# A second attention reordered: q and k first, v in the banks of scores, small work at other places

## The chip, the cores and the metric

The kernel runs on one NeuronCore of a Trainium2 chip. TensorE (PE) multiplies matrices and transposes, VectorE (DVE), ScalarE (ACT) and GpSimd (POOL) work on tiles, and SyncE (SP) only issues DMAs. Each engine takes its instructions in program order, and engines wait for one another by semaphores. SBUF holds tiles of 128 partitions; PE writes to PSUM, eight banks of 128x512 fp32. The metric is the time of one execution on the device in microseconds (us), the median of several.

## The reference

Four layers, each with a residual, on x of 8 sequences of 512 tokens, 256 wide:

```
x = x + attn_a(layernorm(x))     # 16 heads of 64, ALiBi, causal
x = x + ffn(layernorm(x))        # RMS norm, gate, top 2 of 8 experts, swiglu
x = x + attn_b(layernorm(x))     # 8 heads of 128
x = x + ffn(layernorm(x))        # the same weights again

attn_b:  q, k, v = x @ w_aq, x @ w_ak, x @ w_av      # 256 -> 8 heads of 128
         q, k = rope(q), rope(k)                     # rotary positions
         s = q k^T / 128 - 1e30 * (key after query)
         o = softmax(s) v ;   r = o @ w_ao           # 8 heads of 128 -> 256

ffn gate: logits = h @ gate_w.T + gate_b ; vals, idx = top_k(logits, 2)
          wts = softmax(vals)
```

The tokens are then sorted by expert. Only attn_b, the second attention, is changed, and with it the places at which the gate of the layer behind it is computed.

## The kernel before

The program has four stages, one behind the other: `attention_a`, `experts(0)`, `attention_b`, `experts(1)`. In each stage every engine has a function that issues its instructions in an order written out by hand; there is no scheduler. The change lies in `attention_b` (lines 1231 to 1957).

One **unit** is one head of one sequence: u runs from 0 to 63, sequence bt = u // 8, head p = u % 8. I call the units of a sequence its first (p = 0) to its eighth (p = 7). What is done for a head:

- PE `proj_qk` (L1310 to L1312): q (j = 0) and k (j = 1) for 512 tokens, six matmuls each, since every fp32 operand is split into a high and a low part in fp32r. Into bank 0 and bank 1.
- DVE `rope` (L1695 to L1697): three multiplications by the tables out of the bank into `rp`. This frees the bank. POOL `rope` (L1866) adds the two halves into `rf`.
- ACT `high` (L1502) rounds `rf` to the high part, POOL `low` (L1873) takes the rest.
- PE `scores` (L1356 to L1358): four blocks of 128 queries, t = 3 (512 keys) down to t = 0, into banks 2 and 3 in turn; blocks 1 and 0 share the bank of block 3, and wait until DVE has read that.
- DVE `maxima` (L1704): adds the mask, takes the row's maximum, writes P to SBUF. ACT `exps` (L1519), DVE `invert` (L1712), ACT `scale` (L1529), which divides by the sum.
- PE `turn_p` (L1372): P is transposed in three parts, into banks 4 and 5; ACT `copy_p` (L1539) brings each to SBUF.
- PE `attend` (L1387): P times V into bank 6; ACT `heads` (L1545) copies it to `OT`.

The work is pipelined over units. In turn u of the loop PE does the scores of unit u + 1, the transposes of unit u between them, the q and k of unit u + 3, and `attend` of unit u. ACT does in turn u: `copy_p` of u, `high` of u + 2, `exps` and `scale` of u + 1, `heads` of u. DVE does the `maxima` of u + 1 and the `rope` of u + 3, with `invert(u + 1)` between its halves.

Once for four heads PE projects v as well (`proj_v`, L1330 to L1332, four blocks of 128 tokens, six matmuls each, into banks 0 and 1), which ACT copies (L1508). That falls into the second and the sixth unit of a sequence, which are longer on PE by it. In the first unit PE also does `outproj` (L1407) of the sequence before, in two halves through bank 7.

Between these stands the **small work** of a sequence, for the gate of the layer behind it and for the input of the next sequence:

- `residual`, `stats`, `gather_stats`, `normal` on DVE with `deviation` and `mean_square` on POOL: the norms; ACT `gate_in` (L1554, four activations) writes `hh`.
- `gate_turn` (PE, L1282, one part for each half of the features) transposes `hh` into bank 7, ACT `gate_high` (L1561) copies each part, PE `gate_logits` (L1423).
- `top_two` in five pieces (DVE, L202 to L228) and `route` in five (DVE, L264 to L279), with ACT `ratio` (L1574), which the last piece of `top_two` needs; PE `rank`; POOL `put_ids` (L292), four DMAs behind one another, needs the last piece of `route`.
- `xpose` (PE), `x_high` (ACT, L1495) and `x_low` (DVE, L1685): the transposed input of the next sequence. All of `proj_qk` and `proj_v` of that sequence need it; the first of them is the v block in the sixth unit.
- ACT `weigh` (L1569, eight activations) and POOL `combine` (L1859): the layer's input two sequences ahead.

Where the small work stands is set by p in the loops of PE, ACT and POOL. On DVE it is set by a number `at = 7 * p + s` in `between(u, s)`: s = 0 to 3 is behind the four `maxima`, s = 4 behind them, before `rope`, s = 5 and 6 behind `rope`. In the last sequence (bt = 7) the pieces of `listing` and `places` stand there too.

## Time and profile before

| | us |
|---|---|
| median of 3 runs | 2345.34 (2340.38 to 2346.77) |
| the profiled execution, its own time | 2350.32 |
| its span in the trace | 2348.5 |
| PE busy over the span | 2140.3 (91%) |
| DVE busy | 1530.3 (65%) |
| ACT busy | 1453.8 (62%) |
| POOL busy | 1288.9 (55%) |
| the second attention, from the first projection to the first matmul of the experts behind it | 1236.7 to 2056.0 |
| PE's busy time in 100 us of its middle (1657 to 1757) | 93.82 |

The second attention is a bit over a third of the span. A row of the timeline reads: start in us from the span's start, duration, engine, line, operation, tiles; in brackets how long the engine stood idle before it and for whom. The names of tiles are those of the program without their numbers, so `q` stands for all four parts of q and k, `stage` for the transposed gate input, `bank` for any PSUM bank.

### The profile page before, as it was taken

To read this page: it belongs to the slowest core of one execution; us is meant where nothing else is said; L and a number is where in the kernel's file an instruction comes from. 1 tells how busy PE (TensorE), PEld (TensorE's weight loads), DVE (VectorE), ACT (ScalarE), POOL (GpSimd) and SP (SyncE) were. 2 spreads that over 40 slices of the span, in tenths; PEclk is the share of its full clock that TensorE was granted. 3 is DMA by queue.
4 is the path that set the end of the run, shared out by engine and by line. 5 is a ranking of instruction groups with operands and counts; after the bars stand their busy time and mean duration, and the time that the engine had idled before them with its cause. 6 is when DMAs were issued, how large, how long until landed. Compare 5 with 4: busy or idle time off the path is not lost.

```text
span 2348.5 us, 38389 instructions
## 1 busy us (share of the span) xinstructions
PE 2140.3 (91%) x11652; PEld 1722.6 (73%) x11652; DVE 1530.3 (65%) x4317; ACT 1453.8 (62%) x3769; POOL 1288.9 (55%) x1450
## 2 busy tenths in 40 slices
PE   6999999999999999898987999999999999899993
PEld 5677777777777776677875777777777778677882
DVE  5767676767676858466755666656665666656665
ACT  4877676868686868343434776757676575634443
POOL 3665555555555545566643546565665655456661
PEclk8999999999999999999998999999999999899996
DMA  3320000000000001333331001001010000522426
GB/s 124 109 99 28 1 28 1 28 1 28 1 28 1 19 3 69 122 101 100 126 117 37 19 10 37 28 18 46 1 45 28 1 19 3 207 64 72 158 88 237
DMA packets 55140, 132.34 MB, mean 56 GB/s; under 512 B 12256, under 2 KB 30208, under 8 KB 53920
## 3 DMA queue, kind: packets, MB, share of 16 engines
q1 hardware_dynamic: 37216, 92.58, 10.7%
q0 software_dynamic: 17728, 37.32, 5.8%
q8 instruction: 102, 1.67, 0.3%
q14 instruction: 94, 0.77, 0.1%
HBM read 81.51 MB, written 48.35 MB: 55 GB/s over the span
## 4 chain that ended last, share of the span: by engine, by line
PE 59%; DVE 12%; ACT 11%; POOL 8%; issue 6%; DMA 3%; SPq 0%; ACTq 0%; POOLq 0%; DVEq 0%
PE bank L619 5%; PE bank L641 5%; PE bank L2086 4%; PE bank L601 3%; PE bank L1407 3%; PE bank L1387 3%; PE bank L586 2%; PE bank L2060 2%; PE bank L2061 2%; PE bank L2062 2%; ACT P L1519 2%; ACT P L763 2%; PE bank L1372 2%; PE bank L587 2%; ACT P L1529 2%
## 5 line engine op out<-in xcount | busy, mean ns | idle before, releaser
L1107 POOL TENSOR_TENSOR P<-P,rc 128x128 f32<-128x128 f32 (+3 forms) x512 | 355.0, 724 | 361.7 <-DVE rc L929 361.4
L921 DVE CUSTOM_DVE_ANT_0 P<-bank,tab 128x512 f32<-128x512 f32 (+3 forms) x512 | 241.7, 486 | 130.0 <-PE bank L587 126.3
L763 ACT ACTIVATE P<-P,mn 128x128 f32<-128x128 f32 (+3 forms) x512 | 281.5, 552 | 47.7 <-DVE mn L921 44.6
L774 ACT COPY PT<-bank 128x512 f32<-128x512 f32 (+1 forms) x384 | 193.9, 516 | 102.6 <-PE bank L601 95.2
L1873 POOL TENSOR_TENSOR q<-rf,q 128x512 fp32r<-128x512 f32 x128 | 162.4, 1291 | 170.2 <-ACT q L1502 170.1
L1866 POOL TENSOR_TENSOR rf<-rp 128x512 f32<-128x512 f32 x128 | 163.3, 1277 | 165.3 <-DVE rp L1697 161.4
L601 PE MATMUL bank<-cst,P 128*128 128x128 f32 x1280 | 207.8, 277 | 30.3 <-ACT PT L774 16.5
L2290 POOL DMA_INDIRECT yD<-Yf,place x142 | 139.3, 981 | 140.1 <-ACT Yf L2150 128.8
L586 PE MATMUL bank<-q 128*128 128x512 f32 (+3 forms) x512 | 186.7, 375 | 18.8 <-DVE mn L921 14.4
L2136 ACT ACTIVATE sgf<-glf 128x256 f32<-128x256 f32 x142 | 59.3, 418 | 230.3 <-DVE glf L2207 230.3
L601 PEld LDWEIGHTS bank<-cst,P 128*128 128x128 f32 x1280 | 152.8, 141 | 61.3 <-ACT PT L774 21.6
L897 DVE TENSOR_TENSOR q<-bank,q 64x512 fp32r<-64x512 f32 x256 | 175.8, 687 | 8.7 <-ACT q L754 2.6
L310 POOL DMA_INDIRECT Gf<-hD,idx x142 | 138.6, 976 | 67.5 <-issue 40.4
L1519 ACT ACTIVATE P<-P,mn 128x128 f32<-128x128 f32 (+3 forms) x256 | 140.9, 553 | 47.4 <-DVE mn L1704 47.4
L1704 DVE CUSTOM_DVE_ANT_0 P<-bank,tab 128x512 f32<-128x512 f32 (+3 forms) x256 | 117.8, 485 | 72.8 <-PE bank L1358 72.1
L619 PE MATMUL bank<-PT,V 128*64 128x512 f32 (+3 forms) x1024 | 154.4, 444 | 9.1 <-DVE xTl L887 8.2
L754 ACT CAST q<-bank 64x512 fp32r<-64x512 f32 x256 | 146.7, 573 | 13.3 <-PE bank L534 10.2
L587 PE MATMUL bank<-q 128*128 128x512 f32 (+3 forms) x512 | 154.4, 327 | 0.0
L1539 ACT COPY PT<-bank 128x512 f32<-128x512 f32 (+1 forms) x192 | 94.4, 517 | 96.8 <-PE bank L1372 96.1
L1387 PE MATMUL bank<-PT,V 128*128 128x512 f32 (+3 forms) x512 | 152.8, 442 | 0.9 <-ACT PT L1539 0.9
L1529 ACT ACTIVATE P<-P,rc 128x128 f32<-128x128 f32 (+3 forms) x256 | 123.0, 552 | 49.4 <-DVE rc L1712 49.4
L2086 PE MATMUL bank<-W2f,ATf 128*128 x568 | 148.5, 384 | 0.0
(230 smaller groups left out, 6001.4 us busy)
## 6 DMA issues: line engine op xcount, KB each, us to landing
hD<-hh SPq DMA_DIRECT2D x16, 512.0 KB, 2.6
W1lf<-w1lD SPq DMA_DIRECT2D x2, 4096.0 KB, 13.1
yg<-yD SPq DMA_DIRECT2D x14, 512.0 KB, 4.6
X<-in_x SPq DMA_DIRECT2D x8, 512.0 KB, 4.4
stage<-in_w SPq DMA_DIRECT2D x8, 512.0 KB, 3.5
w1hD<-W1A SPq DMA_DIRECT2D x8, 512.0 KB, 2.7
w1lD<-stage SPq DMA_DIRECT2D x8, 512.0 KB, 3.6
rD<-xn SPq DMA_DIRECT2D x8, 512.0 KB, 2.9
```

The source lines that it names most:

```text
L586: e.matmul(o, QS[:, k, hl, ts], KS[:, k, hl, 0:w], start=True, stop=False)
L587: i = e.matmul(o, QS[:, k, hl, ts], KL[:, k, hl, 0:w], start=False, stop=True)
L601: i = e.transpose(o[:, at:at + 128], P[:, h % 3, OFF[t] + cc * 128:OFF[t] + cc * 128 + 128], ident)
L619: i = e.matmul(bank[6][64 * hl:64 * hl + 64, cc * 128:512], V[:, g % 2, cc, col:col + 64], PT[:, hl, PTO[cc]:PTO[cc] + w], start=cc == 0, ...
L763: i = e.activation(ps, ps, ACT.Exp, bias=mn[:, pb, t:t + 1], scale=-1.0, accum_out=rs[:, pb, t:t + 1])
L774: e.copy(PT[:, h % 2, PTO[cs[0]]:PTO[cs[0]] + w], bank[4 + n % 2][:, 0:w]).then_inc(q.a_pt, 1)
L897: e.tensor_tensor(L, bank[j][own, :], H.bitcast(F32), ALU.subtract).then_inc(v_q, 1)
L921: e.tensor_tensor_reduce(out=P[:, pb, OFF[t]:OFF[t] + w], in0=score(h, t), in1=tab[:, 512 - w:512], scale=-SLOPES[h % 16], scalar=3e38, op ...
L1107: i = e.tensor_tensor(ps, ps, rc[:, h % 3, t:t + 1].broadcast_to([128, w]), ALU.mult)
L1387: i = e.matmul(bank[6][:, cc * 128:512], V[:, g % 2, cc, col:col + 128], PT[:, u % 2, PTO[cc]:PTO[cc] + w], start=cc == 0, stop=cc == TT - 1)
L1519: i = e.activation(ps, ps, ACT.Exp, bias=mn[:, pb, t:t + 1], scale=-1.0, accum_out=rs[:, pb, t:t + 1])
L2086: i = e.matmul(o, AT[:, k, kc], W2[:, ex, kc].rearrange("p x n -> p (x n)"), start=False, stop=kc == 1)
```

## The change

The list, in the order of the diff below:

1. **Opening of the stage.** PE first projects q and k of head 0, then v blocks 0 and 1, q and k of head 1, v blocks 2 and 3. These four v blocks go to banks 2, 3, 4 and 5 (`v_bank`), which scores and transposes use later, instead of taking turns in banks 0 and 1; scores and transposes of unit 0 now wait for the copies. ACT copies two v blocks, then `high(0)`, two more, then `high(1)`, which stood behind `exps(0)`. The projection of head 2 and its `rope` stand before the loop, behind the scores of unit 0.
2. **Gate.** `gate_in` goes from the third unit to the second (ACT), `gate_turn(0)` from the fourth unit to the third, `gate_turn(1)` from the end of the fourth unit to between its scores and transposes, `gate_logits` from the fifth unit to the fourth (PE); `gate_high` follows (ACT).
3. **ratio** goes from the fifth unit to the sixth, `weigh` from the second to the first (except in sequence 0).
4. **DVE.** `top_two` 1 to 3 and `route` 0 and 1 go together to `at = 39`, behind the maxima of the sixth unit and before its `invert`; `top_two` 4 to `at = 40`, behind the `rope` of that unit; `route` 2 and 3 together to 46, `route` 4 from 48 to 53, in the eighth unit before its `rope`. `x_low(0)` goes from the end of the fifth unit into the sixth, behind its second maximum, `x_low(1)` behind its fourth. In sequence 0, `normal` goes from 17 and 18 to 24 and 25, one unit later.
5. **POOL.** `deviation` for the input goes from the first unit, behind `put_ids` and `low`, to the eighth unit of the sequence before, ahead of `put_ids`.

```diff
@@ -1300,7 +1305,9 @@
                             e.wait_ge(v_wlo, 12 + SPLIT_AT[2 * j + p // 4])
-                        if u % 4 == 0:
+                        if u == 0:
+                            e.wait_ge(q.v_xT, turned(0, 1))
+                        elif u % 4 == 0:
                             e.wait_ge(a_v, u + 3 + j)
@@ -1320,11 +1327,11 @@
                             e.wait_ge(q.v_xT, turned(bt, 1))
-                        if t > 1:
+                        if g and t > 1:
                             e.wait_ge(a_v, 4 * g + t - 1)
...
                             e.wait_ge(v_rp, 2 * (4 * g - 1) + t + 1)
-                        o, ts = bank[t % 2][:], slice(t * 128, (t + 1) * 128)
+                        o, ts = v_bank(g, t)[:], slice(t * 128, (t + 1) * 128)
                         for kc in range(2):
@@ -1347,6 +1354,8 @@
                             e.wait_ge(p_lo, 2 * u + 2)
+                        if u == 0 and t > 1:
+                            e.wait_ge(a_v, 4 - t)
                         if t == 3 and u:
@@ -1366,6 +1375,8 @@
                             e.wait_ge(q.a_pt, n - 1)
+                        else:
+                            e.wait_ge(a_v, n + 3)
                         at = 0
@@ -1432,10 +1443,17 @@
                                 i.then_inc(q.m_x, 1)
-                    proj(0)
-                    proj(1)
+                    for j in range(2):
+                        proj_qk(0, j)
+                    proj_v(0, 0)
+                    proj_v(0, 1)
+                    for j in range(2):
+                        proj_qk(1, j)
+                    proj_v(0, 2)
+                    proj_v(0, 3)
                     for t in (3, 2, 1, 0):
                         scores(0, t)
+                    proj(2)
                     for u in range(NU):
@@ -1448,9 +1466,9 @@
                                 rank(e, 1, bt - 1)
+                            if p == 3 and bt:
+                                gate_turn(bt - 1, 1)
                             turn_p(u, 0)
-                            if p == 4 and bt:
-                                gate_logits(bt - 1)
                             if p == 5 and nx:
@@ -1462,8 +1480,6 @@
                             outproj(bt - 1, 0)
-                        if u == 0:
-                            proj(2)
                         if u + 3 < NU:
@@ -1474,13 +1490,13 @@
                             pick(e, 1, 0)
-                        if p == 3 and bt:
+                        if p == 2 and bt:
                             if bt == NB - 1:
...
                             gate_turn(bt - 1, 0)
+                        if p == 3 and bt:
+                            gate_logits(bt - 1)
                         attend(u)
-                        if p == 3 and bt:
-                            gate_turn(bt - 1, 1)
                         if p == 4 and nx:
@@ -1576,12 +1592,14 @@
                     x_high(0, 1)
-                    for t in range(TT):
-                        v_copy(0, t)
+                    v_copy(0, 0)
+                    v_copy(0, 1)
                     high(0)
+                    v_copy(0, 2)
+                    v_copy(0, 3)
+                    high(1)
                     exps(0, 0)
                     exps(0, 1)
-                    high(1)
                     scale(0)
@@ -1591,8 +1609,12 @@
                         copy_p(u, 2)
-                        if u and u + 2 < NU:
+                        if p == 3 and bt:
+                            gate_high(bt - 1, 1)
+                        if u + 2 < NU:
                             high(u + 2)
+                        if p == 0 and bt and bt + 2 < NB:
+                            weigh(bt + 2)
                         v = u + 3 < NU and (u + 3) % 4 == 0
@@ -1605,21 +1627,17 @@
                             v_copy((u + 3) // 4, 3)
-                        if u == 0:
-                            high(2)
                         if u + 1 < NU:
                             scale(u + 1)
-                        if p == 4 and bt:
+                        if p == 5 and bt:
                             ratio(bt - 1)
+                        if p == 1 and bt:
+                            gate_in(bt - 1)
                         if p == 2 and bt:
-                            gate_in(bt - 1)
-                        if p == 3 and bt:
                             gate_high(bt - 1, 0)
-                        if p == 1 and bt + 2 < NB:
-                            weigh(bt + 2)
+                        if p == 1 and bt == 0:
+                            weigh(2)
                         heads(u)
-                        if p == 3 and bt:
-                            gate_high(bt - 1, 1)
                         if p == 4 and nx:
@@ -1732,14 +1750,21 @@
                                 normal(1, bt - 1, 2 * (at - 10) + 1)
-                            elif at in (29, 30, 31, 32, 33):
-                                top_two(e, q, at - 29, bt - 1, lg, v8, i8, if8, dv)
-                            elif at == 37:
+                            elif at == 29:
+                                top_two(e, q, 0, bt - 1, lg, v8, i8, if8, dv)
+                            elif at == 39:
+                                for n in (1, 2, 3):
+                                    top_two(e, q, n, bt - 1, lg, v8, i8, if8, dv)
                                 route(e, q, 1, bt - 1, 0)
+                                route(e, q, 1, bt - 1, 1)
                             elif at == 40:
-                                route(e, q, 1, bt - 1, 1)
-                            elif at in (46, 47, 48):
-                                route(e, q, 1, bt - 1, at - 44)
+                                top_two(e, q, 4, bt - 1, lg, v8, i8, if8, dv)
+                            elif at == 46:
+                                route(e, q, 1, bt - 1, 2)
+                                route(e, q, 1, bt - 1, 3)
+                            elif at == 53:
+                                route(e, q, 1, bt - 1, 4)
                         if bt == NB - 1:
@@ -1762,9 +1787,9 @@
                                 gather_stats(0, 1)
-                            elif at in (17, 18):
-                                normal(0, 1, 2 * (at - 17))
-                                normal(0, 1, 2 * (at - 17) + 1)
+                            elif at in (24, 25):
+                                normal(0, 1, 2 * (at - 24))
+                                normal(0, 1, 2 * (at - 24) + 1)
@@ -1783,21 +1808,20 @@
                     invert(0)
+                    rope(2, 0)
+                    rope(2, 1)
                     for u in range(NU):
...
                                 maxima(u + 1, t)
-                                if p == 5 and nx and t == 2:
-                                    x_low(bt + 1, 1)
+                                if p == 5 and nx and t in (2, 0):
+                                    x_low(bt + 1, 1 - t // 2)
                                 between(u, 3 - t)
...
                             residual(bt - 1, 0)
-                        if u == 0:
-                            rope(2, 0)
-                            rope(2, 1)
@@ -1881,16 +1903,12 @@
                     low(1)
+                    rope(2, 0)
+                    rope(2, 1)
                     for u in range(NU):
                         bt, p = divmod(u, 8)
-                        if u and u + 2 < NU:
+                        if u + 2 < NU:
                             low(u + 2)
-                        if p == 0 and bt and bt + 1 < NB:
-                            deviation(0, bt + 1)
-                        if u == 0:
-                            rope(2, 0)
-                            rope(2, 1)
-                            low(2)
                         if p == 2 and bt == 0:
@@ -1906,6 +1924,8 @@
                                 gather(e, 1, q, a)
+                        if p == 7 and bt + 2 < NB:
+                            deviation(0, bt + 2)
                         if p == 7 and bt and bt + 1 < NB:
...
                                 put_ids(e, 1, bt - 1, n)
```

The rows below are the instructions of one engine in the order of the program, numbered, with the tiles they write and read and their shapes.

ACT at the opening of the stage; `xTh` is the transposed input, `q_1` q and k, `P` the scores. Before:

```order
1308 L1495 CAST xTh<-bank 128x512 x2
1309 L1508 COPY V<-bank 128x512 x4
1310 L1502 CAST q_1<-rf 128x512 x2
1311 L1519 ACT_TABLE_LOAD
1312 L1519 ACTIVATE P,rs<-P,mn 128x128
1313 L1519 ACTIVATE P,rs<-P,mn 128x256
1314 L1519 ACTIVATE P,rs<-P,mn 128x384
1315 L1519 ACTIVATE P,rs<-P,mn 128x512
1316 L1502 CAST q_1<-rf 128x512 x2
1317 L1529 ACTIVATE P<-P,rc 128x128
```

Now:

```order
1308 L1511 CAST xTh<-bank 128x512 x2
1309 L1524 COPY V<-bank 128x512 x2
1310 L1518 CAST q_1<-rf 128x512 x2
1311 L1524 COPY V<-bank 128x512 x2
1312 L1518 CAST q_1<-rf 128x512 x2
1313 L1535 ACT_TABLE_LOAD
1314 L1535 ACTIVATE P,rs<-P,mn 128x128
1315 L1535 ACTIVATE P,rs<-P,mn 128x256
1316 L1535 ACTIVATE P,rs<-P,mn 128x384
1317 L1535 ACTIVATE P,rs<-P,mn 128x512
1318 L1545 ACTIVATE P<-P,rc 128x128
```

The casts for head 1 stand ahead of the exponentials of head 0 now, and two copies of v behind the casts for head 0.

ACT from the last activation of `scale` in the third unit of a middle sequence; `hh` and `stage` are the gate's, `OT` is `heads`, `PT` is `copy_p`. Before:

```order
1904 L1529 ACTIVATE P<-P,rc 128x384
1905 L1529 ACTIVATE P<-P,rc 128x512
1906 L1554 ACTIVATE hh<-xl,r_1 128x256 x4
1907 L1545 COPY OT<-bank 128x512
1908 L1539 COPY PT<-bank 128x512 x2
1909 L1539 COPY PT<-bank 128x256
1910 L1502 CAST q_1<-rf 128x512 x2
```

Now:

```order
1906 L1545 ACTIVATE P<-P,rc 128x384
1907 L1545 ACTIVATE P<-P,rc 128x512
1908 L1577 COPY stage<-bank 128x512
1909 L1561 COPY OT<-bank 128x512
1910 L1555 COPY PT<-bank 128x512 x2
1911 L1555 COPY PT<-bank 128x256
1912 L1577 COPY stage<-bank 128x512
1913 L1518 CAST q_1<-rf 128x512 x2
```

The four activations into `hh` are gone from here (they stand one unit earlier), and the two copies into `stage` stand here, where they stood one unit later.

DVE in the sixth unit; `xTl` is `x_low`, `P,mn` a maximum, `w` the last piece of `top_two`, `M` and `Ms` the routing tables, `rc` is `invert`. Before, from the end of the fifth unit:

```order
2983 L224 TENSOR_SCALAR w<-dv 128x4
2984 L226 RECIPROCAL w<-w 128x4
2985 L228 TENSOR_TENSOR w<-w,dv 128x4
2986 L1685 TENSOR_TENSOR xTl<-bank,xTh 128x512
2987 L1704 ISA P,mn<-bank,tab 128x512
2988 L1704 ISA mn 128x1
2989 L1704 ISA P,mn<-bank,tab 128x384
2990 L1704 ISA mn 128x1
2991 L1685 TENSOR_TENSOR xTl<-bank,xTh 128x512
2992 L1704 ISA P,mn<-bank,tab 128x256
2993 L1704 ISA mn 128x1
2994 L264 TENSOR_TENSOR Ms<-M 128x32
```

Now, from the fourth maximum of the sixth unit:

```order
2988 L1722 ISA P,mn<-bank,tab 128x128
2989 L1722 ISA mn 128x1
2990 L1703 TENSOR_TENSOR xTl<-bank,xTh 128x512
2991 L208 MAX v_1<-lg 128x8 x4
2992 L212 MAX_INDEX i_1<-v_1,lg 128x8 x4
2993 L215 CAST if_1<-i_1 128x32
2994 L216 TENSOR_TENSOR dv<-v_1 128x4
2995 L219 TENSOR_TENSOR M<-cst,if_1 128x4x8
2996 L220 TENSOR_TENSOR M<-cst,if_1 128x4x8
2997 L264 TENSOR_TENSOR Ms<-M 128x32
2998 L267 TENSOR_REDUCE Ms<-Ms 128x8
2999 L1730 RECIPROCAL rc<-rs 128x4
```

Nothing stands ahead of the first maximum of the sixth unit any more; the second `x_low` has moved from behind the second maximum to behind the fourth.

## Rows read from the trace of the kernel before

**Rows 1.** Windows, by stretch: duration, busy us per engine, PEclk, DMA share, GB/s.

```profile
1306.00:1312.00 6.00, 4.45 (x19) 4.26 (x20) 3.32 (x11) 3.97 (x9) 1.95 (x2) 0.50 0.00 0
1657.00:1757.00 100.00, 93.82 (x490) 76.71 (x489) 62.63 (x173) 67.35 (x169) 60.14 (x58) 1.00 0.08 27
```

**Rows 2.** Waits, 1370 to 2020: total us, times, longest us.

```profile
PE bank L1356 <- DVE mn L1704: 15.9, 14, 1.5
...
PE bank L1282 <- ACT stage L1561: 9.4, 7, 3.0
...
PE bank L1372 <- ACT P L1529: 8.1, 6, 1.4
...
PE bank L1407 <- DVE X L1717: 3.4, 5, 0.7
```

**Rows 3.** Timeline, one middle sequence: where PE stood idle, with the releaser.

```profile
1771.49 0.70 PE L1407 MATMUL bank<-WO,OT 128*128 128x256 f32 x2 [0.68 <-DVE X L1717]
...
1805.59 0.44 PE L1372 MATMUL bank<-cst,P 128*128 128x128 f32 x2 [0.75 <-ACT PT L1539]
...
1812.44 0.63 PE L1282 MATMUL bank<-cst,hh 128*128 128x128 f32 x4 [1.05 <-ACT stage L1561]
...
1825.74 0.66 PE L1372 MATMUL bank<-cst,P 128*128 128x128 f32 x4 [1.35 <-ACT P L1529]
...
1828.77 0.38 PE L1356 MATMUL bank<-q 128*128 128x256 f32 x1 [1.50 <-DVE mn L1704]
...
1852.47 0.38 PE L1356 MATMUL bank<-q 128*128 128x256 f32 x1 [0.84 <-DVE mn L1704]
```

**Rows 4.** Timeline, the same sequence: small work that stood ahead of those releasers.

```profile
1769.24 0.73 DVE L1680 TENSOR_SCALAR xn<-X,mv,rstd 128x256 f32<-128x256 f32 x2 [7.89 <-POOL rstd L1824]
...
1802.89 1.70 ACT L1554 ACTIVATE hh<-xl,r 128x256 f32<-128x256 f32 x4
...
1825.82 1.28 DVE L224 TENSOR_SCALAR w<-dv 128x4 f32<-128x4 f32 x1
...
1850.73 1.09 DVE L279 CAST dI<-dF 128x8 int32<-128x8 f32 x1
```

**Rows 5.** Timeline, the opening of the stage.

```profile
1236.73 0.47 PE L1330 MATMUL bank<-WhB,xTh 128*128 128x512 f32 x1 [2.06 <-DVE xTl L1685]
...
1245.45 0.69 DVE L1695 TENSOR_TENSOR rp<-bank,tab 128x512 f32<-128x512 f32 x1 [8.87 <-PE bank L1312]
...
1251.00 2.49 POOL L1873 TENSOR_TENSOR q<-rf,q 128x512 fp32r<-128x512 f32 x2
...
1253.64 0.47 PE L1356 MATMUL bank<-q 128*128 128x512 f32 x1 [2.26 <-POOL q L1873]
...
1263.08 0.77 PE L1356 MATMUL bank<-q 128*128 128x512 f32 x1 [6.18 <-issue]
...
1275.82 2.32 PE L1387 MATMUL bank<-PT,V 128*128 128x512 f32 x8
```

**Rows 6.** Timeline: the fourth unit of sequence 0, and the last sequence.

```profile
1307.55 1.97 PE L1372 MATMUL bank<-cst,P 128*128 128x128 f32 x8 [4.37 <-ACT P L1529]
...
2015.98 1.09 PE L1282 MATMUL bank<-cst,hh 128*128 128x128 f32 x4 [3.00 <-ACT stage L1561]
...
2030.67 1.09 PE L1372 MATMUL bank<-cst,P 128*128 128x128 f32 x8 [1.78 <-ACT P L1529]
```

**Rows 7.** Timeline, the sixth unit: the v block, what it waits for, and its end.

```profile
1829.11 0.69 DVE L1685 TENSOR_TENSOR xTl<-bank,xTh 128x512 fp32r<-128x512 f32 x1
...
1829.85 0.50 PE L1330 MATMUL bank<-WhB,xTh 128*128 128x512 f32 x1
...
1830.17 0.28 DVE L1704 CUSTOM_DVE_ANT_0 P<-bank,tab 128x128 f32<-128x128 f32 x1
...
1838.23 2.32 PE L1387 MATMUL bank<-PT,V 128*128 128x512 f32 x8
```

**Rows 8.** The page: one group of a line; its mean is in ns.

```profile
L1519 ACT ACTIVATE P<-P,mn 128x128 f32<-128x128 f32 (+3 forms) x256 | 140.9, 553 | 47.4 <-DVE mn L1704 47.4
```

More of the change, by code:

```diff
@@ L258, in route @@
             if piece == 0:
-                e.wait_ge(q.v_top, 11 * bt + 10)
+                e.wait_ge(q.v_top, 11 * bt + 11)
                 if s > 1:
@@ L1272, in score, with v_bank @@
                     return o[:, 256:384] if t == 0 else o[:, 0:(t + 1) * 128]
+                def v_bank(g, t):
+                    return bank[t % 2] if g else bank[2 + t]
                 def experts_over(e):
@@ L1507, in v_copy @@
                             e.wait_ge(q.m_o, 4 * g - 4)
-                        e.copy(V[:, g % 2, t], bank[t % 2][:]).then_inc(a_v, 1)
+                        e.copy(V[:, g % 2, t], v_bank(g, t)[:]).then_inc(a_v, 1)
                     def exps(u, half):
@@ L1813, in vector @@
                         between(u, 6)
-                        if p == 4 and nx:
-                            x_low(bt + 1, 0)
                     return residual, stats, gather_stats, normal, (lg, v8, i8, if8, dv)
```

## The prediction, made before the changed kernel was run

> **What bounds the kernel now.** I read the windows of the second attention first, then PE's waits there, then the timeline of one sequence with all engines. In the middle of the stage PE is busy 93.82 of 100 us at full clock [rows 1], so only its idle time can go: some 6 us for each sequence. PE's waits from 1370 to 2020 say who ends it: 15.9 + 9.4 + 8.1 + 3.4 = 36.8 us in four rows [rows 2], and six times 0.75 of the next group makes 41.3, nearly all of it. The timeline shows the same six gaps in every middle sequence: 0.68 at the second half of `outproj`, 0.75 in the fourth unit before the third part of the transposes, 1.05 at `gate_turn(1)`, 1.35 and 1.50 in the sixth, 0.84 in the eighth: 6.17 us [rows 3]. Just ahead of the releasers stands small work: `gate_in` 1.70, `top_two` 4 1.28, `route` 4 1.09, and a `normal` for which DVE stood 7.89 us until POOL had done `put_ids`, `low` and `deviation` [rows 4]. Two more places are large: the opening, where PE's first scores come at 1253.64, 16.9 us after its first projection, and head 1's scores only at 1263.08 after 6.18 idle [rows 5]; and a gap of 4.37 in sequence 0 [rows 6], behind which the granted clock is 0.50, which is 1.2 GHz [rows 1].
>
> **The change, a middle sequence.** PE's work is the same; what counts is which gaps close and open.
> - *Gate.* `gate_in` goes into the second unit, where PE has v and q,k: 36 matmuls in 8.38 us (1829.85 to 1838.23 shows the like in the sixth unit, [rows 7]) against 2.8 for q,k alone, so ACT has more room than the 1.70. The 0.75 goes. `gate_high(0)` then stands behind the third unit's `scale`, some 0.5 us, and `gate_turn(1)` meets it after the next two scores, with about 0.1 to spare: the 1.05 goes. If that margin fails, 0.2 comes back. Gain 1.80.
> - *Sixth unit, relieved.* `top_two` leaves the fifth, so `invert` there is no longer late, nor is the first maximum of the sixth: 1.35 + 1.50 = 2.85 go. The whole block (`top_two` 1 to 3, `route` 0 and 1) now stands before an `invert` for which the exponentials are ready only after v's four blocks. I expect 3.9 to 4.5 us of work in some 7 us of waiting: free.
> - *Sixth unit, a new wait.* The v block needs `x_low(1)`, and this now comes behind the fourth maximum. That ended at 1830.45; plus 0.69 is 1831.14, against v's start at 1829.85 [rows 7]: 1.3 later. The maxima need the scores, and v follows these directly, so it is not hidden. Cost 1.3 (bounds 0.7, one `x_low`, and 2.0).
> - *Seventh unit.* `top_two` 4 stands behind the `rope` of the sixth and ahead of the seventh's first maximum, 1.6 us with its two small followers; `rank` (1 us of PE) covers most. Cost 0.1 (0 to 0.5).
> - *Eighth unit.* `route` 4 leaves it before the first maximum: the 0.84 goes. But it comes back before `rope`, with two of the four `stats` around it, and at that time POOL is in `low`, so I take the 1.09 of the row [rows 4], not less. `rope` is 1.05 late, `invert` 0.85 after what it waited for, and PE's transposes in the next first unit come 0.88 late; the second half of `rope` with `gather_stats` delays the next first maximum by another 0.27. Cost 1.15 (0 if the cast is short, 1.5 at most), in five sequences; without `stats` (sequence 6) it fits.
> - *First unit.* `deviation` runs ahead of `put_ids`, so DVE doesn't stand 7.89, `residual` is on time, the 0.68 goes (five times, [rows 2]). `put_ids` and `low` come 1.4 us later; scores need that `low` only after both halves of `outproj`, over 10 us behind. `weigh`, 3.3 us on ACT, lies beside the first half of `outproj`, 7 us of PE. Free; if the rows it scales were not there yet, it would cost: their DMA is issued half a sequence earlier.
>
> Sum for sequences 1 to 5: 1.80 + 2.85 - 1.3 - 0.1 + 0.84 - 1.15 + 0.68 = 3.62, times 5 = 18.1. Sequence 6, without the 1.15 and the 0.68: 4.1.
>
> **Price of a small DVE operation.** `top_two` 4's first instruction takes 1.28 [rows 4] for 4 elements a partition, and it started just behind a POOL addition. The Trainium skill (SBUF — State Buffer, Who interferes with whom) says that DVE and GpSimd share a pair of ports, and that whoever starts first holds it for the whole instruction. By the row the piece costs 1.28 at its new place too; by the rule it is short there, since both wait for the same `rope` and DVE goes on first, and the 0.1 of the seventh unit would be nothing: 0.7 us less in all.
>
> **The change, sequence 0.** *Opening.* The first projection stays at 1236.73. `rope` started at 1245.45, after 30 matmuls; now after six, at about 1239.5. Four halves of `rope`, 3 x 0.69 each, follow the projections, to 1249.6; POOL adds (taken as long as its `low`, 2.49 for two, [rows 5]), ACT casts, POOL's two `low` of head 0 end by 1247.7. PE has 48 matmuls, at 8.38/36 = 0.233 each 11.2 us, and 1.5 more for the part at half clock (30 took 8.5, not 7.0): 1249.4. So scores at 1249.4, not 1253.64. Head 0 goes on through its maxima (behind `rope`, to 1252.8), exponentials (4 x 0.553, [rows 8], after a table load), `invert`, `scale` to first transposes at 1257.4; PE has the projection of head 2 and the scores of head 1 in between and idles 1.4. Then the first maximum of head 1 stands behind head 2's `rope` (two halves, 4.2 us from 1255.5): 2.2 idle. `attend(0)` comes at 1264.3, not 1275.82 [rows 5]: 11.5. I take off 1.5 for half clock behind these gaps (the scores at 1263.08 take 0.77 for 0.47 [rows 5]), and 1.0 for `combine`, which falls together with the next maxima: 9 (bounds 5 and 12).
> *Fourth unit.* `normal` moves a unit later, when POOL's `deviation` is done: 4.37 goes [rows 6], and the half clock behind it, half of the 4.45 us that PE works in that stretch [rows 1], so 2.2; less 0.1 for `normal` ahead of a `rope`: 6.5. *Sixth unit.* No gate work there; the v wait costs 1.1.
> Sum: 9 + 6.5 - 1.1 = 14.4.
>
> **Last sequence.** 3.00 before `gate_turn(1)` and 1.78 in the sixth unit [rows 6], 1.4 behind that, and stretches at half clock. The places leave the `listing` on DVE; of the 3.00 about 1.1 stays as a wait for the first maximum of the fifth unit. The three last units have no projections and hang on ACT and DVE, not PE; there the block of `top_two` costs DVE some back. I take 6 (2 to 9).
>
> **Sum.** 18.1 + 4.1 + 14.4 + 6 = 42.6. The profiled execution took 2350.3 (span 2348.5 and 1.8 around it), so 2307.7; it lies 5.0 above the median of 2345.3, so 2302.7: **2303**.
>
> **Rivals.**
> - *The waits only move.* ACT and DVE are busy 67.35 and 62.63 of 100 us [rows 1], but their work of a plain unit comes in chains close behind PE's, so small work that leaves one place finds no room at another, and middle sequences keep their 6.17. For it: two of my own terms (1.3, 1.15) are such. Against it: three of the pieces go to units with v or `outproj`. Then only the opening, the fourth unit of sequence 0 and half of the last sequence count: 9 + 6.5 + 3 = 18.5, 2327.
> - *The new wait halves the clock.* The wait ahead of v is the place: if PE falls to half clock there, 36 matmuls (8.38 us, [rows 7]) take 8.4 more, in seven sequences 59, less 42.6: 2362, slower. It decides once it happens in five of seven. For it: 0.50 after 4.37 idle [rows 1, 6]. Against it: 1.35 and 1.50 within 3 us at the same place [rows 3], each as long as the new wait, leave the clock at 1.00 over all of 1657 to 1757 [rows 1]. The Trainium skill (TensorE: Matmul & The Clock Gate, What's actually happening) says the clock is set by how busy PE has lately been; with that, fewer idle us speak for a faster clock here.
> - *The opening gives nothing back.* POOL's chain for heads 1 and 2 takes the time, or `combine`, which now meets `rope`: 9 becomes 2, 2310. That is inside my range.
>
> **Chances.** The forecast with its terms 0.85; waits only move 0.10; half clock 0.03; something that I haven't seen and that costs all of it 0.02. All terms at their good ends (12, 9, no 1.15 and 0.1, v wait 0.7) (and nothing in the eighth unit) give 2286; all bad ends (5, 2, v wait 2.0, 0.5, 1.5, and 0.2 back at the gate) give 2321. Range 2291 to 2324, which leaves out part of the second case and the third. Against a bound of 0.3% (7 us), which is about what a measurement tells from no change: faster 0.94, same 0.03, slower 0.03.
>
> **What would show it.** In the profile after, each middle sequence keeps only: about 1.3 before the v block of the sixth unit, released by DVE's `x_low`, and about 0.9 and 0.3 at the first unit's transposes and scores. Gone: `stage`, `PT` and `X` as releasers of PE, and DVE's 7.89 for `rstd`. The first scores near 1249, the first `attend` near 1265, no stretch at 0.50 near 1300. A middle sequence is 3.6 us shorter. I am wrong if PE still idles 6 us a sequence, or the clock drops at the v block.

## The result, and the profile after

| | before | after |
|---|---|---|
| median of the runs, us | 2346.06 (4 runs) | 2288.87 (2284.78 to 2290.96, 4 runs) |
| ratio, 95% interval | | 0.9758 (0.9737 to 0.978) |
| the profiled execution | 2350.32 | 2289.44 |

The changed kernel is 57.2 us faster by the medians; I had forecast 42.6, and its time lies 2 us below my range. The profiled executions differ by 60.9; the one of before lay 4.3 above its median, the one of after 0.6. The starts of PE's first score matmul of each unit cut this up. All is in us; the first row gives a point in time, the others the lengths of stretches:

| stretch | before | after | gained | forecast |
|---|---|---|---|---|
| start of the first projection | 1236.73 | 1234.17 | 2.6 | 0 |
| from there to the scores of head 4 | 64.98 | 55.10 | 9.9 | 9 |
| rest of sequence 0 | 53.46 | 49.27 | 4.2 | 5.4 |
| sequences 1 to 6 | 603.66 | 566.17 | 37.5 | 22.2 |
| last sequence, to the first matmul of the experts | 97.19 | 90.45 | 6.7 | 6 |

The code ahead of the first projection is the same in both kernels, and on another chip the same start came 2 us later with the change (1248.1 to 1248.7 in e10 to e12) than without it (1246.2 in e9), so the 2.6 is not counted as the change's. The miss is in sequences 1 to 6. The windows of the changed kernel, 100 us of its middle and the time at which the kernel before ran at half clock (columns as in [rows 1], to which they answer):

```profile
1606.00:1706.00 100.00, 98.90 (x531) 82.40 (x530) 67.19 (x188) 71.45 (x178) 63.24 (x59) 1.00 0.10 34
1306.00:1312.00 6.00, 5.23 (x37) 4.50 (x35) 4.90 (x14) 5.25 (x12) 2.56 (x2) 1.00 0.00 0
```

PE is busy 98.90 where it had been busy 93.82, and the clock is 1.00 where it was 0.50. The changed kernel is further on in the program at 1306; the transposes that had stood behind the 4.37 of [rows 6] are these, without a wait, and the granted clock is 1.00 from 1270 to 1320:

```profile
1290.58 1.03 PE L1383 MATMUL bank<-cst,P 128*128 128x128 f32 x8
```

The timeline of PE in a middle sequence after: the nine starts that bound its eight units, and between them the only wait that is left, with the `x_low` that ends it (this answers to [rows 3] and [rows 7]):

```profile
1716.51 0.48 PE L1365 MATMUL bank<-q 128*128 128x512 f32 x1
1738.35 0.48 PE L1365 MATMUL bank<-q 128*128 128x512 f32 x1
1751.73 0.48 PE L1365 MATMUL bank<-q 128*128 128x512 f32 x1
1760.07 0.48 PE L1365 MATMUL bank<-q 128*128 128x512 f32 x1
1770.23 0.48 PE L1365 MATMUL bank<-q 128*128 128x512 f32 x1
1778.56 0.48 PE L1365 MATMUL bank<-q 128*128 128x512 f32 x1
...
1782.58 0.69 DVE L1703 TENSOR_TENSOR xTl<-bank,xTh 128x512 fp32r<-128x512 f32 x1
1783.32 0.50 PE L1337 MATMUL bank<-WhB,xTh 128*128 128x512 f32 x1 [1.10 <-DVE xTl L1703]
...
1793.72 0.48 PE L1365 MATMUL bank<-q 128*128 128x512 f32 x1
1802.70 0.48 PE L1365 MATMUL bank<-q 128*128 128x512 f32 x1
1810.61 0.48 PE L1365 MATMUL bank<-q 128*128 128x512 f32 x1
```

The eight units take 21.84, 13.38, 8.34, 10.16, 8.33, 15.16, 8.98, 7.91, in sum 94.1. Before they took 22.82, 13.38, 7.89, 10.98, 10.09, 17.39, 8.98, 9.01, in sum 100.5. But for the third units of sequences 2 to 4 and a few single ones, these times repeat to 0.1 from one middle sequence to the next and from one execution to the next, so they show what a median over runs can't. A middle sequence is 6.4 shorter, not 3.6. The small work at its new places (this answers to [rows 4]):

```profile
1794.74 0.17 DVE L224 TENSOR_SCALAR w<-dv 128x4 f32<-128x4 f32 x1
1794.78 1.27 POOL L1888 TENSOR_TENSOR rf<-rp 128x512 f32<-128x512 f32 x1 [0.85 <-DVE rp L1715]
...
1806.94 2.56 POOL L1895 TENSOR_TENSOR q<-rf,q 128x512 fp32r<-128x512 f32 x2 [1.71 <-ACT q L1518]
1806.95 0.15 DVE L279 CAST dI<-dF 128x8 int32<-128x8 f32 x1
...
1807.36 0.69 DVE L1713 TENSOR_TENSOR rp<-bank,tab 128x512 f32<-128x512 f32 x1
```

The cast of `route` 4, the last piece of it, for which I had taken 1.09, took 0.15 in five sequences and 0.17 in the sixth; `rope` is not late behind it, and the next first unit has no gap at all. The first instruction of `top_two` 4 took 0.17, not 1.28. The opening and the fifth unit of sequence 0 (this answers to [rows 5] and [rows 6]):

```profile
1234.17 0.76 PE L1317 MATMUL bank<-xTh,WhB 128*128 128x512 f32 x1 [2.06 <-DVE xTl L1703]
1237.11 0.69 DVE L1713 TENSOR_TENSOR rp<-bank,tab 128x512 f32<-128x512 f32 x1 [3.08 <-PE bank L1319]
1247.96 0.39 PE L1365 MATMUL bank<-q 128*128 128x512 f32 x1
...
1256.14 1.09 PE L1383 MATMUL bank<-cst,P 128*128 128x128 f32 x8 [1.65 <-ACT P L1545]
1259.05 0.39 PE L1365 MATMUL bank<-q 128*128 128x256 f32 x1 [1.81 <-DVE mn L1722]
1264.37 2.32 PE L1398 MATMUL bank<-PT,V 128*128 128x512 f32 x8
...
1292.86 3.39 DVE L1698 TENSOR_SCALAR xn<-X,mv,rstd 128x256 f32<-128x256 f32 x4
1293.51 2.59 POOL L1895 TENSOR_TENSOR q<-rf,q 128x512 fp32r<-128x512 f32 x2 [1.50 <-ACT q L1518]
...
1300.46 1.09 PE L1383 MATMUL bank<-cst,P 128*128 128x128 f32 x8 [1.81 <-ACT P L1545]
```

The two waits of the opening are there, 1.65 (forecast 1.4) and 1.81 (2.2). The first `attend` stands at 1264.37 where I had 1264.3, but the stage began 2.6 earlier than I had taken. Counted from the first projection the first scores come after 13.8 (forecast 12.7, before 16.9) and the first `attend` after 30.2 (forecast 27.6, before 39.1): 1.1 and 2.6 later than forecast. The clock was 0.50 until 1240. And `normal` at its new place takes 3.39 for four, not 1.5, and leaves 1.81 of PE's wait one unit later.

### The profile page after: what moved, and what is told of

The parts are those of the page before. It is cut to its first block, busy times and chain, and to the rows that moved or that the text cites. A ratio compares the mean times of both kernels' runs of the same rounds, so it can differ in the third digit from the quotient of the medians.

```text
span 2287.6 us, 38390 instructions
## 1 busy us (share of the span) xinstructions
PE 2121.5 (93%) x11652; PEld 1715.9 (75%) x11652; DVE 1525.0 (67%) x4317; ACT 1454.2 (64%) x3769; POOL 1291.6 (56%) x1450
## 4 chain that ended last, share of the span: by engine, by line
PE 71%; DVE 9%; ACT 6%; POOL 6%; issue 4%; DMA 3%; SPq 0%; another core or an unknown queue 0%; ACTq 0%; POOLq 0%; DVEq 0%
PE bank L1398 5%; PE bank L619 5%; PE bank L1418 5%; PE bank L641 5%; PE bank L2106 4%; PE bank L601 4%; PE bank L1383 3%; PE bank L1317 2%; PE bank L1319 2%; PE bank L586 2%; PE bank L2081 2%; PE bank L2080 2%; PE bank L1318 2%; PE bank L2082 2%; ACT P L763 2%
## 5 line engine op out<-in xcount | busy, mean ns | idle before, releaser
L763 ACT ACTIVATE P<-P,mn 128x128 f32<-128x128 f32 (+3 forms) x512 | 281.6, 552 | 47.4 <-DVE mn L921 44.3
L754 ACT CAST q<-bank 64x512 fp32r<-64x512 f32 x256 | 146.7, 573 | 12.7 <-PE bank L534 9.5
L292 POOL DMA_INDIRECT slotD<-cst,dI x128 | 126.6, 989 | 38.0 <-issue 35.2
```

Of the source, the lines that this page charges most:

```text
L763: i = e.activation(ps, ps, ACT.Exp, bias=mn[:, pb, t:t + 1], scale=-1.0, accum_out=rs[:, pb, t:t + 1])
```

## The experiments

On the chips used the kernel before took 2345 to 2404 us, so a run is compared by its ratio to the kernel before on its own chip, and edits of a few us by their unit times in the trace. The edits are shown shortened, with the places that move and not every line; unless it is said otherwise they are edits of the changed kernel. The changed kernel again, beside e2 to e4:

> The changed kernel once more, beside the next three on one chip. All theories: 0.976 of the kernel before, as measured; it gives the base against which edits of a few us are read.

Measured: 0.9765 (0.9743 to 0.9786). Units as above; 94.1 in sequences 1, 4, 5 and 6.

**The cast of `route` 4.** e3 changes the order of two DVE instructions in the eighth unit:

```diff
-    elif at == 53: route(e, q, 1, bt - 1, 4)      # ahead of stats(0, bt + 2, 3)
+    if at == 53: stats(0, bt + 2, 3); route(e, q, 1, bt - 1, 4)
```

> In the eighth unit the fourth stats and the last piece of route (one cast of 8 elements a partition) change places on DVE; nothing else. In the changed kernel the cast starts within 0.01 us of POOL's low and takes 0.15 us, where my forecast had 1.09. Theory A (the small cast is held up while POOL is inside an instruction of its own): now it starts 0.4 us after POOL's low has begun, and takes 0.8 to 1.0; rope, invert and the transposes of the next first unit come 0.75 late, and with 0.25 of extra cost the five sequences lose 4 to 5 us. Rival B (the cast is short at this place whatever POOL does, or the delay has slack): 0, within 1 us, and a cast of 0.15.

Measured: ratio 0.9771 (0.9753 to 0.9789). DVE and POOL in the eighth unit of e3:

```profile
1818.67 2.54 POOL L1897 TENSOR_TENSOR q<-rf,q 128x512 fp32r<-128x512 f32 x2 [1.71 <-ACT q L1518]
1819.01 0.98 DVE L279 CAST dI<-dF 128x8 int32<-128x8 f32 x1
1819.91 0.68 DVE L1713 TENSOR_TENSOR rp<-bank,tab 128x512 f32<-128x512 f32 x1
```

The cast now starts 0.34 behind POOL's first `low` and ends with it (1818.67 + 1.27 = 1819.94; 1819.99). It took 0.98 in the five sequences in which stats stands ahead of it and 0.17 in the sixth, which has none. So DVE is held until POOL is done, in all five, and theory A stands in kind; but the next first unit takes 22.51 instead of 21.86, 0.65 more and not 1.0. My 1.15 would have been too much even with the cast held.

e4 puts the cast back behind the `rope` of the seventh unit, e13 the reduction of `route` 3 as well:

```diff
-    elif at == 46: route 2, route 3
-    elif at == 53: route 4
+    elif at == 46: route 2, route 3     # e4
+    elif at == 48: route 4
+    elif at in (46, 47, 48): route 2, 3, 4 one by one     # e13
```

> The last piece of route back behind the rope of the seventh unit, all else as changed. Theory A: the cast takes 1.09 there again, PE gets back the 0.84 gap in the eighth unit and 0.26 behind it: 1.1 in six sequences, 6.6 us slower than the changed kernel. Rival B (idle column alone): 5.0. My forecast's terms (0.84 against 1.15) would make this kernel 0.7 us faster than the changed one.

> Pieces 3 and 4 of route (a reduction and the cast) back behind the rope of the seventh unit, where the kernel before has them; all else as changed. With the cast alone put back it stood directly behind rope, started 0.05 us before POOL's addition, took 0.17 and cost nothing. Theory J (the reduction of 0.22 ahead of it lets POOL start first, and the cast then lasts until POOL's addition ends): cast 1.09, a gap of 0.84 in the eighth unit, 9.01 instead of 7.91 for it, in six sequences, 6.6 us slower than the changed kernel by the trace. Rival K (the gap had its cause elsewhere, in top_two or stats): 7.91 stays.

Measured: e4 0.9749 (0.9729 to 0.9768), eighth unit 7.91: all three expectations of it fell; by the unit times the edit costs nothing. e13 0.9785 (0.9752 to 0.9818), eighth unit 9.01 to 9.03 in all six sequences, as theory J has it to 0.02. The two timelines at the end of the `rope`, e4 first:

```profile
1815.61 0.68 DVE L1715 TENSOR_TENSOR rp<-bank,tab 64x512 f32<-64x512 f32 x1
1816.33 0.17 DVE L279 CAST dI<-dF 128x8 int32<-128x8 f32 x1
1816.38 1.28 POOL L1888 TENSOR_TENSOR rf<-rp 128x512 f32<-128x512 f32 x1 [1.04 <-DVE rp L1715]
```

and, at the same place, the kernel before, in which the cast of [rows 4] follows at 1850.73 (e13 has the same cast of 1.09):

```profile
1850.47 0.22 DVE L274 TENSOR_REDUCE dF<-pr 128x8 f32<-128x64 f32 x1
1850.52 1.27 POOL L1866 TENSOR_TENSOR rf<-rp 128x512 f32<-128x512 f32 x1 [1.05 <-DVE rp L1697]
```

Directly behind `rope` the cast starts 0.05 ahead of POOL's addition and is short; with 0.22 of other work in front it starts 0.21 behind it and lasts until POOL is done (1850.52 + 1.27 = 1851.79; 1851.82). To close the gap of 0.84 it was enough that the reduction left (e4); whether moving the cast alone would have done it, no run shows. The Trainium skill (SBUF — State Buffer, Who interferes with whom) says that issue order, and not the shape of an operation, decides which of DVE and GpSimd is blocked, and for the whole instruction. Three places of the cast agree: started 0.05 ahead of POOL 0.17, 0.21 behind 1.09, 0.34 behind 0.98. So does `top_two` 4, whose first instruction took 0.17 at its new place, 0.04 ahead of POOL, and 1.28 at the old one, 0.03 behind:

```profile
1825.79 1.27 POOL L1866 TENSOR_TENSOR rf<-rp 128x512 f32<-128x512 f32 x1 [0.91 <-DVE rp L1697]
1825.82 1.28 DVE L224 TENSOR_SCALAR w<-dv 128x4 f32<-128x4 f32 x1
```

The cast of the changed kernel, 0.01 behind by the rows and yet 0.15 long, is too close to say by the rows who was first.

**What a gap costs.** e7 puts `deviation` back:

```diff
-    if p == 7 and bt + 2 < NB: deviation(0, bt + 2)
+    if p == 0 and bt and bt + 1 < NB: deviation(0, bt + 1)
```

> POOL's deviation back in the first unit, behind put_ids and low; all else as changed. The forecast's term: 0.68 in five sequences, 3.4 us slower than the changed kernel. Theory A (0.30 more for each gap): 4.9. Rival C (residual is on time in any case since put_ids has moved): 0.

Measured: 0.9788 (0.9757 to 0.9819), first unit 22.80 to 22.82 against 21.86 in five sequences: 0.95 each, 4.8 in all, as theory A. PE in e7, the last projection matmul and the second half of `outproj`, then the same in e1:

```profile
1759.00 0.39 PE L1319 MATMUL bank<-xTh,WlB 128*128 128x512 f32 x1
1760.08 7.17 PE L1418 MATMUL bank<-WO,OT 128*128 128x256 f32 x32 [0.69 <-DVE X L1735]
```

```profile
1741.59 0.39 PE L1318 MATMUL bank<-xTl,WhB 128*128 128x512 f32 x1
1741.82 0.39 PE L1319 MATMUL bank<-xTh,WlB 128*128 128x512 f32 x1
1742.05 7.07 PE L1418 MATMUL bank<-WO,OT 128*128 128x256 f32 x32
```

A projection matmul starts every 0.23 but its row is 0.39 long. The idle column counts from the end of the row, so a wait of 0.69 moves the next start from 0.23 to 1.08 behind the last, 0.85; the half of `outproj` behind it takes 7.17 instead of 7.07. The Trainium skill (Perfetto Trace Analysis, Summary: the profiler window per engine type) says that the end of a TensorE row is an estimate; the overlap of the rows agrees. Both x_low earlier, e2:

```diff
-    if p == 5 and nx and t in (2, 0): x_low(bt + 1, 1 - t // 2)
+    if p == 5 and nx and t > 1: x_low(bt + 1, 3 - t)
```

> The two x_low of the sixth unit stand behind its first and second maximum, not behind the second and fourth. In the changed kernel PE waits 1.10 us for the second x_low ahead of v in each of seven sequences, the only wait left there. Theory A (a gap costs more than its idle time, because PE's first matmuls behind it run longer too: unit times fell by 0.26 to 0.48 more than the idle columns): the v block starts at the end of the last transposes, and each sequence is 1.1 + 0.25 shorter, 9.5 us in all. Rival B (only the idle column counts): 7.7 us. Rival C (x_low now waits on DVE for ACT's x_high, and the maxima behind it make scores or transposes late): nothing gained, a new gap of about 1 us released by DVE's maximum.

Measured: 0.9739 (0.9712 to 0.9765), sixth unit 14.21 to 14.26 against 15.14 to 15.21: 0.95 in seven sequences, 6.6, less than either expectation. The second `x_low` of e2 waits for ACT's `x_high`, and v still waits for it, 0.14 by the rows:

```profile
1786.59 0.69 DVE L1703 TENSOR_TENSOR xTl<-bank,xTh 128x512 fp32r<-128x512 f32 x1 [0.22 <-ACT xTh L1511]
1786.79 0.41 PE L1383 MATMUL bank<-cst,P 128*128 128x128 f32 x2
1787.34 0.50 PE L1337 MATMUL bank<-WhB,xTh 128*128 128x512 f32 x1
```

In the second unit v waits for nothing. The changed kernel there, and in its sixth unit (the v block behind the last row is the one at 1783.32 above):

```profile
1741.18 0.41 PE L1383 MATMUL bank<-cst,P 128*128 128x128 f32 x2
1741.34 0.48 PE L1337 MATMUL bank<-WhB,xTh 128*128 128x512 f32 x1
...
1781.82 0.41 PE L1383 MATMUL bank<-cst,P 128*128 128x128 f32 x2
```

Start to start, v comes 0.16 behind the transposes without a wait, 0.55 in e2 and 1.50 in the changed kernel. So the wait of 1.10 costs 1.34 here, near theory A's 1.35; e2 took away 0.95 of that and left 0.39, and the two idle columns (1.10 - 0.14 = 0.96) agree with the 0.95 only because both hide the same 0.24. e2 can't decide between A and B, since its v still waits. Theory A's size stands here and in e7, its reason (slower matmuls behind the gap) for 0.1 only: most of what the column hides is the overlap of the rows.

**The other parts, one by one.** e5 puts the gate back, e6 the sixth unit (`top_two`, `ratio`, `route` 0 and 1, `x_low`):

```diff
-    p == 1: gate_in; p == 2: gate_turn(0), gate_high(0); p == 3: gate_turn(1), gate_high(1), gate_logits
+    p == 2: gate_in; p == 3: gate_turn(0), gate_high(0), gate_turn(1), gate_high(1); p == 4: gate_logits
```

```diff
-    at 39: top_two 1 to 3, route 0, 1;  at 40: top_two 4;  p == 5: ratio, x_low(0), x_low(1)
+    at 30 to 33: top_two 1 to 4;  at 37, 40: route 0, 1;  p == 4: ratio, x_low(0);  p == 5: x_low(1)
```

> The gate's input, its two transposes, their copies and the logits back at their places of the kernel before; all else as changed. The forecast's term is 1.80 in each of sequences 1 to 6, 10.8, and about 2 in the last: 13 us slower than the changed kernel. Theory A (each gap costs some 0.2 more than its idle time): units three to five of a middle sequence fell by 2.13, so 12.8 and 2 to 3 in the last: 15. Rival C (the waits only moved; ACT finds its room elsewhere): under 3 us.

> top_two 1 to 4, ratio, route 0 and 1 and both x_low back at their places of the kernel before; all else as changed. The forecast's terms (2.85 less 1.3 less 0.1, in six sequences, less 1.1 in sequence 0) make it 7.6 us slower than the changed kernel, with something in the last sequence. Theory A (gaps cost more than their idle time, the v wait is 1.10, the 0.1 is nothing): the sixth unit fell by 2.23, so 13.4, less 0.65 in sequence 0: 13, with something in the last sequence. Rival C: under 3.

Measured: e5 0.9841 (0.9813 to 0.9868), a sequence without other waits 96.3 against 94.1, 2.2 times 6 = 13.3. The last one takes 80.15 against 70.12 up to the scores of its last head, and 99.2 against 89.1 up to the first matmul of the experts: 10, where 2 to 3 were expected. e6 0.9814 (0.9785 to 0.9842), sixth unit 17.3 against 15.2 and the sequence 96.3 against 94.1, in six sequences 13.1, less 0.65 in sequence 0. In the last one it takes 4.4 more up to the scores of the last head, but only 1.1 more up to the first matmul of the experts (90.1 against 89.1 in e1, and 90.5 in the first trace of the changed kernel): what lies between is 3.3 shorter without the change. In the middle both agree with theory A. In e5 the waits of before are back, the 0.76 and the 1.07 of its sequence 5:

```profile
1806.35 0.44 PE L1383 MATMUL bank<-cst,P 128*128 128x128 f32 x2 [0.76 <-ACT PT L1555]
...
1813.22 0.63 PE L1287 MATMUL bank<-cst,hh 128*128 128x128 f32 x4 [1.07 <-ACT stage L1577]
```

e8 puts `normal` of sequence 0 back; e10 is the kernel before with the opening alone:

```diff
-    elif at in (24, 25): normal(0, 1, ...)
+    elif at in (17, 18): normal(0, 1, ...)
```

> In sequence 0 normal back one unit earlier; all else as changed. The forecast's term: 6.5 us slower than the changed kernel (the gap of 4.37 and half clock behind it). By the changed kernel's trace normal costs about 2.0 at its new place, a gap of 1.81 in the fifth unit released by ACT's scale, so undoing gives 6.9 less 2.0: 4.9 slower. Rival C (the opening runs earlier now, so that POOL's chain no longer makes normal late): 0 or faster by 2.

> The kernel before with the opening of the stage alone changed (q and k first, v in the banks of scores and transposes, head 2 sooner). The forecast's term: 9 us faster (bounds 5 and 12). By the traces: the stretch from the first projection to the scores of head 4 went from 64.98 to 55.10 us, 9.9 faster, if nothing of it is given back behind. Rival (the opening gives nothing back): 2 faster.

Measured: e8 0.9782 (0.9755 to 0.9809); fourth unit 15.38 against 7.92, fifth 8.35 against 10.37: 5.4 together, between the two expectations. e10 0.9963 (0.9943 to 0.9983), with 54.59 from the first projection to the scores of head 4, against 64.98 in the first trace of before and 66.41 in that on its own chip (e9): 10.4 to 11.8, inside my bounds 5 and 12, nothing given back; by the ratio it is 8.9 (4 to 14).

**Better versions.** e11 and e14 have e2's `x_low`, and the second pair of `normal` further on:

```diff
-    elif at in (24, 25): normal(0, 1, ...) two each
+    elif at in (24, 27): normal(0, 1, ...) two each     # e11, behind rope
+    elif at in (24, 31): normal(0, 1, ...) two each     # e14, ahead of the next rope
```

> The changed kernel with both x_low behind the first and second maximum of the sixth unit (as measured alone: 0.95 us in each of seven sequences, 6.6), and in sequence 0 the second pair of normal behind rope of the fourth unit instead of before it. Theory F (the 1.81 gap in the fifth unit of sequence 0 is the second pair ahead of rope, 0.7, and what follows from it): the fifth unit takes 8.4 instead of 10.37, 2 us, 8.6 in all against the changed kernel, ratio 0.973. Rival G (normal behind rope makes the next first maximum late by as much): 6.6 in all, with a gap released by DVE's maximum in the fifth unit.

> Both x_low behind the first and second maximum of the sixth unit, and in sequence 0 the second pair of normal a whole unit later, between the last maximum and the rope of the fifth unit. Theory F: with one pair (0.74) ahead of each rope both fit into DVE's wait for the projection, and the fifth unit takes 8.4 instead of 10.37 (9.90 with the pair behind rope): 8.6 us less than the changed kernel in all. Rival G (a pair is held by POOL's low and lasts 1.5 or more wherever it stands in that unit): the wait turns up in the fifth or sixth unit, 6.6 to 7 in all.

Measured: e11 0.9701 (0.9677 to 0.9724), fifth unit 9.90, rival G, with a new wait of 1.31 for DVE's maximum. e14 0.9713 (0.9685 to 0.9742), fifth unit 8.35, theory F to 0.05. Where e14's pairs stand, and e11's second:

```profile
1289.06 0.73 DVE L1698 TENSOR_SCALAR xn<-X,mv,rstd 128x256 f32<-128x256 f32 x2
1296.97 0.73 DVE L1698 TENSOR_SCALAR xn<-X,mv,rstd 128x256 f32<-128x256 f32 x2
```

```profile
1312.97 1.79 DVE L1698 TENSOR_SCALAR xn<-X,mv,rstd 128x256 f32<-128x256 f32 x2
1313.01 1.27 POOL L1888 TENSOR_TENSOR rf<-rp 128x512 f32<-128x512 f32 x1 [1.05 <-DVE rp L1715]
```

A pair takes 0.73 while POOL is idle and is done before its next instruction; four in a row run into `low` (3.39 in the changed kernel), and so does a pair that POOL's addition overtakes (1.79). Both kernels beat the changed one by their unit times; of the ratios' intervals e11's lies below the changed kernel's of 0.9743 to 0.9786 (e1) and e14's ends close to it, so they don't rank the two. e14 is the better by its trace: its middle sequence takes 93.2, its sequence 0 from first projection 100.45 against 104.4.

**A wait that I had not seen.** In the trace of the changed kernel the third unit of sequence 2 takes 9.80, in e1 11.08, in e7 15.51, in e13 8.34. DVE and ACT stand there for something that the profile puts outside the core's engines (`remote`); e1:

```profile
1479.85 0.69 DVE L1713 TENSOR_TENSOR rp<-bank,tab 128x512 f32<-128x512 f32 x1 [3.06 <-remote]
1479.94 0.58 ACT L1561 COPY OT<-bank 128x512 f32<-128x512 f32 x1 [2.24 <-remote]
```

In e1 the 512 KB store of `hh` runs at that time. e9 is the kernel before, unchanged, and e12 is e11 with a wait on SP:

```diff
     e.wait_ge(q.a_h, bt + 1)
+    if bt < NB - 2: e.wait_ge(q.a_o, 8 * bt + 12)
     e.dma_start(hDv[1][bt], hh[:])
```

> The kernel before, traced on the chip of the next three. In the traces of the changed kernel DVE's rope in the third unit of sequences 2 to 4 is held for 1.8 to 5.6 us by nothing in the core (remote), while the 512 KB store of hh is under way; the first trace of the kernel before has no such wait. Theory D (the wait came with the change, which moved gate_in and so the store one unit earlier): all third units 7.9 us here, and this chip's kernel before is as long in the attention as on the first. Rival E (it belongs to the chip and the execution): third units of over 8.5 us here too.

> The last one, and the store of hh (SP) waits until the copy of head 4 is done, two units later, in all sequences but the last two. Theory H (what holds DVE and ACT in the third unit is a fetch of instructions behind the store's 0.5 MB): third units of 8.34 in every sequence, 1.5 to 8 us less than the kernel without the late store by the trace; the same wait may turn up elsewhere where a fetch meets the store. Rival I (the store has no part in it): third units over 9 us in sequence 2 as before, same time.

Measured: e9 2397.3 us, with third units of 13.24 and 9.82 in sequences 2 and 3: the wait is not the change's (rival E). e12 0.9708 (0.9682 to 0.9734), with 14.61 and 10.34 there, and a window around the wait in which DMA moves 1 GB/s (its last number), so no store, though DVE waits 3.70:

```profile
1470.00:1484.00 14.00, 11.93 (x56) 9.31 (x54) 5.36 (x11) 10.29 (x25) 6.94 (x9) 1.00 0.01 1
```

```profile
1482.15 0.69 DVE L1713 TENSOR_TENSOR rp<-bank,tab 128x512 f32<-128x512 f32 x1 [3.70 <-remote]
```

So the store has no part in it either (rival I). In e1, e7, e9 and e12 the DMA view shows one 16 KB packet of the queue for instructions 3 to 6 us ahead of the end of that wait. But such a packet stands at the same place of the program in e13 (1466.6) and in the first trace of before (1489.2), which have no wait there. So that DVE waits for it is not shown.

## Why the prediction was wrong in size

- *What bounds the kernel, and which gaps go:* right. All six gaps of [rows 3] are gone, and 1.10 is left at v where I had 1.3. e5, e6, e7 and e13 bring them back, two, two, one and one. "The waits only move" and "half clock" fell: PE is busy 98.90 of 100 at 1.00.
- *The eighth unit, "cost 1.15":* the step that failed first. I took the cast's 1.09 from [rows 4] for the new place since POOL would be in `low`. DVE came 0.01 us behind POOL by the rows, the cast took 0.15, and the step cost 0. Five times 1.15 = 5.75 us. And had it been held, it would have cost 0.65 (e3). The end "0 if the cast is short" stood in my bounds; the value I took was wrong.
- *Every gap at its idle column:* the step that failed with the larger sum. First unit 0.96 for 0.68, units three to five 2.13 for 1.80, sixth 3.3 for 2.85 (17.39 against 15.16 less v's new 1.10), eighth 1.11 for 0.84: 7.5 for 6.17. The column leaves out 0.17 to 0.28 a gap, since the rows of PE overlap. (The first unit's gap stands in sequences 2 to 6, not 1 to 5 as I had it, which leaves the sum as it is.) Over sequences 1 to 6 that is 0.28 x 5 + 0.33 x 6 + 0.46 x 6 + 0.27 x 6 = 7.8 us, half of the miss of 15.3 in that stretch.
- *The small costs:* v's wait 1.10 for 1.3 and the seventh unit nothing for 0.1: 6 x 0.3 = 1.8. With 5.75 and 7.8 that is 15.3. Two accidents of one execution each cancel: in the trace of before the sixth unit of sequence 2 ran 1.5 longer (the granted clock from 1519 to 1540 was 0.92), in that of after its third unit by 1.5.
- *The eighth unit's gain of 0.84:* the gap went as forecast, but the cast need not have moved for it: without the reduction in front it is short at its old place too (e4, e13).
- *Opening:* 9.9 for 9, by luck in its parts. Up to the first `attend` it gained 8.9 and not 11.5, and of the 2.5 that I took off behind that nothing was lost; another 1.0 was gained there. *Fourth unit of sequence 0:* 4.2 with v's wait for 5.4; "less 0.1 for `normal` ahead of a `rope`" was 2.0, since the second pair ran into POOL's `low`.
- *Last sequence:* 6.7 for 6, by luck in its parts. Up to the scores of the last head it became 10.7 shorter, and what is behind them, without projections, took back 4.0. Undone singly up to the same scores the gate costs 10.0 and the sixth unit 4.4 (e5, e6); of the 4.4 the last stretch gives back 3.3. What is behind those scores differs by execution: 17.1 to 20.3 in the twelve traces with the sixth unit changed (20.3 in this one), 15.4 to 16.3 in the four without. So the 6.7 is good to some 3 us.
- *`top_two` 4, weighed against the Trainium skill (SBUF — State Buffer, Who interferes with whom):* its first instruction took 0.17, as by the rule, not the row's 1.28, and the seventh unit lost nothing. In the eighth unit I took the row as well, and there too who starts first was the question.

## What to carry to other kernels

Price a gap by the distance of two starts with and without it, not by the idle column: it hid 0.2 to 0.3 us per gap here, 1.3 us of 7.5 in a sequence. The duration of the small DVE operations seen here, a cast and a TENSOR_SCALAR on SBUF, went by who started first, DVE or POOL, so don't carry it from its old place to the new one; put it directly behind the DVE instruction that releases POOL (0.17), and not one instruction later (1.09). And read in a repeated program the times of its units rather than the medians: they repeated to 0.1 us where the intervals of the runs were 4 us and more to either side.

## What was not expected of the hardware

- One reduction of 0.22 us ahead of a cast cost PE 1.10 us a sequence (e4 against e13).
- Four `normal` took 3.39 together and 1.46 in two separate pairs.
- In the third unit of sequences 2 to 4 DVE and ACT stand up to 5.6 and 4.7 us for something that the profile doesn't show (e7), differently in each execution, with any order of the kernel; its cause stays open.
